# A graph network on one core: the order within a tick of the node sweeps

## The chip, the core and the metric
The kernel runs on one core of one Trainium2 chip. A core has five engines with a queue of instructions each: TensorE (matmuls; PE, and PEld for its weight loads), VectorE (DVE), ScalarE (ACT), GpSimd (POOL) and SyncE (SP, transfers only). They meet only through semaphores. The metric is the device time of one execution in microseconds; less is better. Three runs of the kernel before gave 10204.31, 10207.6 and 10220.76 us.

## The reference
Node features x [6250, 64] and 200000 edges go through four residual blocks, each `x = x + block(h)` with `h = relu(layernorm(x))`. The first block is a message-passing network of three layers:

```python
def _ffn(x, w, b):
    return jax.nn.relu(_ln(x @ w + b))
for l in range(3):
    m = concatenate([x[dst], x[src], edge_features])
    m = _ffn(m, msg_w1[l], msg_b1[l])
    m = _ffn(m, msg_w2[l], msg_b2[l])
    agg = segment_sum(m, dst)
    x = x + _ffn(concatenate([x, agg]), upd_w[l], upd_b[l])
```

The other blocks are a gated graph convolution with a batch norm, a plain sum over neighbours, and a linear message with a linear read-out. The change concerns the last line of the loop above, the update of the nodes.

## The kernel before
Nodes lie in SBUF as 49 windows of 128 nodes: H (the block's x), ACC (the aggregate) and X (the outer x), each [128, 49, 64] in float32. The kernel is a row of stages with a barrier between them. Edge work is done in spread stages and message passes; between them stand the node sweeps. node_sweep(l) is called four times: l = 0 (no update), l = 1 and 2 after the first and second message pass, and l = 3 after the third, ahead of the gate. In the texts the last three are sweeps 1, 2 and 3. The windows are cut into 7 chunks, six of 8 windows and one of a single window.

A sweep is a software pipeline whose order is written out by hand. In tick T each engine runs the pieces of its function `tick` in the order of the code, and `part(lag)` gives chunk T - lag, or nothing if there is none. The links of one chunk are:

- TensorE turns H and ACC (L1613, lag 0); ScalarE copies both out of PSUM (L1669, lag LU = 1); TensorE multiplies them with the update's weights (L1636, lag 1); VectorE adds the bias into t_pre (L1725, lag 1, two instructions, "the update's sums").
- With lag LA = 2: ScalarE squares t_pre (L1684), VectorE sums the squares of a row (L1730), ScalarE takes the root (L1686), VectorE the reciprocal (L1732) and the relu with its scale (L1735), GpSimd adds the result to H (L1797).
- In sweep 3 only, lag LN = 3: GpSimd has added H to X (L1800), and VectorE and ScalarE normalize X into H (L1742, L1744, L1746, L1693, L1749, L1695, L1751, L1753).
- TensorE turns the new H; ScalarE copies it (L1676); TensorE multiplies it with the next stage's weights (L1622, "table products"); VectorE adds the bias (L1768, "table sums"); ScalarE, GpSimd and VectorE split the result into three bf16 pieces (L1712 first, L1809 and L1699 second, L1760 third). Sweep 3 does the same for a second table (L1708, L1776, L1702, L1814).

t_pre and relu have two buffers each. The square goes into `stage`, which is one buffer for both norms, so a square waits until the earlier row sum has read it. up_ps, the update's product, has one buffer.

Of the kernel before, what the change touches and what calls it, by code (L numbers as in the profile page):

```python
# [10 lines left out]
ALU = mybir.AluOpType  # L11
ACT = mybir.ActivationFunctionType
# [5 lines left out]
D = 64  # L18
E16, E32 = 16, 32
HID = 128  # L20
LAYERS = 3
# [34 lines left out]
def build(nc, x, src, dst, ea16, ea32, w1, b1, w2, b2, wu, bu, wf, bf, ws, bs, gamma, beta, v1_in, c1, v2, c2, out):  # L56
# [23 lines left out]
    with ctx:  # L80
# [37 lines left out]
        biases = sb("biases", [P, 3 * LAYERS, D])  # L118
# [61 lines left out]
        def at_least(eng, s, value, scale=1):  # L180

            if isinstance(value, int) and value <= 0:
                return
            eng.wait_ge(s, value * scale)
# [1354 lines left out]
        def node_sweep(l, far=None, loads=None):  # L1539

            update, normed, gate = l > 0, l in (0, LAYERS), l == LAYERS
            width = 2 * D
            LU, LA, LN = 1, 2, 3 if update else 0
# [7 lines left out]
            with ExitStack() as stack:  # L1551
                def tiles(name, shape, dt=F32, slots=2):
                    return [stack.enter_context(nc.sbuf_tensor(f"{name}{h}_n{l}", shape, dt)) for h in range(slots)]

                s = {n: sem(f"node_{n}_n{l}") for n in (
                    "h_turned", "acc_turned", "h_t", "acc_t", "updated", "t", "t_square", "t_sum", "t_root", "t_rec", "relu",
                    "h_next", "x_next", "x_sum", "x_mean", "x_centre", "x_square", "x_sum2", "x_root", "x_rec", "h", "hn_turned",
                    "hn_t", "near", "near_in", "near0", "near_rest", "near1", "near2", "far", "far0", "far_in", "far1", "far2",
                    "zeroed")}
                if update:  # L1560
                    h_t, acc_t = tiles("h_t", [P, WIN // 2, P]), tiles("acc_t", [P, WIN // 2, P])
                    t_pre, relu = tiles("t_pre", [P, WIN, D]), tiles("relu", [P, WIN, D])
# [11 lines left out]
                def windows_of(i):  # L1574
                    a, b = CHUNKS[i]
                    return slice(a, b), b - a

                def sides(nw):

                    return [(e, (nw + 1 - e) // 2) for e in range(2) if nw > e]  # L1580
# [12 lines left out]
                def over_windows(v, n, f):  # L1593
                    return v.rearrange("p (a f) -> p a f", a=1).broadcast_to([P, n, f])
# [65 lines left out]
                @block.scalar  # L1660
                def _(act):
                    def tick(part):
                        if update and (i := part(LU)) is not None:
                            at, nw = windows_of(i)
                            cols, deep = (nw + 1) // 2, min(nw, 2) * D
                            for side, ps, turned, done in ((h_t, h_ps, "h_turned", "h_t"), (acc_t, acc_ps, "acc_turned", "acc_t")):
                                act.wait_ge(s[turned], i + 1)
                                at_least(act, s["updated"], i - 1)
                                act.activation(side[i % 2][0:deep, 0:cols, :].rearrange("p k n -> p (k n)"), ps[0:deep, 0:cols * P],  # L1669
                                               ACT.Copy).then_inc(s[done], 1)  # L1670
                        if (i := part(LB)) is not None:
                            at, nw = windows_of(i)
                            cols, deep = (nw + 1) // 2, min(nw, 2) * D
                            act.wait_ge(s["hn_turned"], i + 1)
                            at_least(act, s["far" if gate else "near"], i - 1)
                            act.activation(hn_t[i % 2][0:deep, 0:cols, :].rearrange("p k n -> p (k n)"), hn_ps[0:deep, 0:cols * P],  # L1676
                                           ACT.Copy).then_inc(s["hn_t"], 1)
                        if update and (i := part(LA)) is not None:
                            at, nw = windows_of(i)
                            act.wait_ge(s["t"], 2 * i + len(sides(nw)))  # L1680
                            at_least(act, s["t_sum"], i)
                            if normed:
                                at_least(act, s["x_sum2"], i - 1)
                            act.activation(square[:, 0:nw, :], t_pre[i % 2][:, 0:nw, :], ACT.Square).then_inc(s["t_square"], 1)  # L1684
                            act.wait_ge(s["t_sum"], i + 1)
                            act.activation(t_size[:, at], t_size[:, at], ACT.Sqrt, bias=eps[:], scale=1.0 / D).then_inc(s["t_root"], 1)  # L1686
                        if normed and (i := part(LN)) is not None:
                            at, nw = windows_of(i)
                            act.wait_ge(s["x_centre"], i + 1)
                            at_least(act, s["x_sum2"], i)  # L1690
                            if update:
                                act.wait_ge(s["t_sum"], min(i + 2, len(CHUNKS)))
                            act.activation(square[:, 0:nw, :], centre[:, 0:nw, :], ACT.Square).then_inc(s["x_square"], 1)  # L1693
                            act.wait_ge(s["x_sum2"], i + 1)
                            act.activation(x_size[:, at], x_size[:, at], ACT.Sqrt, bias=eps[:], scale=1.0 / D).then_inc(s["x_root"], 1)  # L1695
                        if (i := part(LB + 2)) is not None:
                            at, nw = windows_of(i)
                            act.wait_ge(s["near_rest"], i + 1)
                            act.activation(piece(at, 1), halves(near_rest[i % 2], nw), ACT.Copy).then_inc(s["near1"], 1)  # L1699
                            if gate:  # L1700
                                act.wait_ge(s["far_in"], 2 * i + len(sides(nw)))
                                act.activation(NEARB[:, at, 1, :], far_rest[i % 2][:, 0:nw, :], ACT.Copy).then_inc(s["far1"], 1)  # L1702
                        if (i := part(LB)) is not None:
                            at, nw = windows_of(i)
                            if gate:
                                act.wait_ge(s["far"], i + 1)
                                for e, n in sides(nw):
                                    act.activation(NEARB[:, at.start + e:at.stop:2, 0, :],  # L1708
                                                   far_ps[e][:, 0:n * width].rearrange("p (k f) -> p k f", f=width),
                                                   ACT.Copy).then_inc(s["far0"], 1)  # L1710
                            act.wait_ge(s["near_in"], 2 * i + len(sides(nw)))
                            act.activation(piece(at, 0), halves(near_sum[i % 2], nw), ACT.Copy).then_inc(s["near0"], 1)  # L1712

                    ticks(tick)

                @block.vector
                def _(dve):
                    def tick(part):
                        if update and (i := part(LU)) is not None:
                            at, nw = windows_of(i)  # L1720
                            dve.wait_ge(s["updated"], i + 1)
                            at_least(dve, s["relu"], i - 1)
                            at_least(dve, s["t_square"], i - 1)
                            for e, n in sides(nw):
                                dve.tensor_tensor(t_pre[i % 2][:, e:nw:2, :], up_ps[e][:, 0:n * D].rearrange("p (k f) -> p k f", f=D),  # L1725
                                                  over_windows(biases[:, 2 * LAYERS + l - 1, :], n, D), ALU.add).then_inc(s["t"], 1)
                        if update and (i := part(LA)) is not None:
                            at, nw = windows_of(i)
                            dve.wait_ge(s["t_square"], i + 1)
                            dve.tensor_reduce(t_size[:, at], square[:, 0:nw, :], AX, ALU.add).then_inc(s["t_sum"], 1)  # L1730
                            dve.wait_ge(s["t_root"], i + 1)
                            dve.reciprocal(t_size[:, at], t_size[:, at]).then_inc(s["t_rec"], 1)  # L1732
                            dve.wait_ge(s["t_rec"], i + 1)
                            at_least(dve, s["h_next"], i - 1)
                            dve.scalar_tensor_tensor(out=relu[i % 2][:, 0:nw, :], in0=t_pre[i % 2][:, 0:nw, :], scalar=0.0,  # L1735
                                                     in1=by_window(t_size[:, at], nw), op0=ALU.max,
                                                     op1=ALU.mult).then_inc(s["relu"], 1)
                        if normed and (i := part(LN)) is not None:
                            at, nw = windows_of(i)
                            if update:  # L1740
# [1042 lines left out]
```

## Time and profile before

| | us |
|---|---|
| median of three runs | 10207.6 |
| profiled execution | 10204.8 |
| its span | 10203.1 |
| TensorE busy | 7656.1 (75%) |
| GpSimd busy | 7272.0 (71%) |
| VectorE busy | 6637.9 (65%) |
| ScalarE busy | 6204.9 (61%) |

The profile is one execution. The span runs from its first to its last instruction. Busy shares are means over all stages. An engine's idle time is put down to what ended it. The mean granted clock of TensorE over the whole span is 0.809 of 2.4 GHz.

### The profile page before, as it was taken

The numbers are of one execution on the slowest core, as the hardware profiler recorded it, in microseconds if no ns is written. First come the engines' busy times: TensorE is split into PE (matmuls) and PEld (weight loads), VectorE is DVE, ScalarE is ACT, GpSimd is POOL, SyncE is SP. The second block draws the span as 40 slices with busy tenths as digits, with TensorE's granted clock in tenths as the row PEclk, the third lists the DMA queues.
The fourth block names the chain that finished last, engine by engine and source line by source line (L and its number), as shares of the span: only waits on it lengthen the run. The fifth ranks groups of instructions, "written<-read, shape, count | busy, mean of one in ns | idle before, by whom it ended". The sixth has DMA issues, their size and how long they took to land. (4 is left out here: it accounts for less than half of the span.)

```text
span 10203.1 us, 372978 instructions
## 1 busy us (share of the span) xinstructions
PE 7656.1 (75%) x123409; PEld 6557.4 (64%) x123409; DVE 6637.9 (65%) x16063; ACT 6204.9 (61%) x15877; POOL 7272.0 (71%) x10039
## 2 busy tenths in 40 slices
PE   6666666645568999978999899996888866545666
PEld 5444444434457788878888788886766656445666
DVE  7444444456645888835888358884399993664697
ACT  2555555546535999926999369983388872443343
POOL 2777777777756888846887468874589975775676
PEclk8555555556589999989999899997999989557887
DMA  5111111149998777768777687777998869667887
GB/s 229 56 56 56 59 56 55 56 131 289 284 259 299 231 237 236 231 239 290 235 230 209 248 287 235 230 204 202 385 279 270 270 184 360 209 207 241 301 255 195
DMA packets 1598119, 2189.50 MB, mean 215 GB/s; under 512 B 508971, under 2 KB 1110844, under 8 KB 1583294
## 3 DMA queue, kind: packets, MB, share of 16 engines
q1 hardware_dynamic: 1275038, 1195.71, 39.0%
q0 software_dynamic: 210528, 491.24, 17.4%
q10 hardware_dynamic: 112320, 499.48, 12.3%
q8 instruction: 141, 2.31, 0.1%
q14 instruction: 92, 0.75, 0.0%
HBM read 1245.73 MB, written 827.61 MB: 203 GB/s over the span
## 5 line engine op out<-in xcount | busy, mean ns | idle before, releaser
L636 POOL DMA_INDIRECT by_src<-sort_rec,slots x1560 | 1534.5, 984 | 650.1 <-issue 649.5
L1306 POOL DMA_INDIRECT NEAR<-spread_f,gather_ids_l x1368 | 1351.7, 988 | 252.2 <-issue 173.8
L1432 ACT ACTIVATE z_l<-z_l,sizes_l 128x64 f32<-128x64 f32 x5472 | 1375.8, 341 | 0.0
L770 PE MATMUL bank<-hots_t 104*128 104x512 bf16 (+3 forms) x1568 | 610.0, 464 | 720.1 <-ACT junk L597 719.4
L770 PEld LDWEIGHTS bank<-hots_t 104*128 104x128 bf16 x1568 | 216.5, 138 | 1017.7 <-ACT junk L597 830.8
L1516 PE MATMUL bank<-wm_diag,zr_t_l 128*128 128x128 f32 x5472 | 794.1, 288 | 0.0
L1516 PEld LDWEIGHTS bank<-wm_diag,zr_t_l 128*128 128x128 f32 x5472 | 663.6, 191 | 155.7 <-issue 155.7
L1469 PE MATMUL bank<-m_l,hot_wide_l 128*128 128x64 f32 x5472 | 744.3, 279 | 0.0
L1149 POOL COPY unit_near_a<-NEARB 128x192 bf16 x1368 | 417.4, 351 | 430.1 <-PE bank_bf L1134 221.8
L1495 PE MATMUL bank<-near_of_l,hot_t_l 128*128 128x64 bf16 x16416 | 600.8, 194 | 97.4 <-issue 54.2
L1469 PEld LDWEIGHTS bank<-m_l,hot_wide_l 128*128 128x128 f32 x5472 | 667.6, 192 | 0.0
L1495 PEld LDWEIGHTS bank<-near_of_l,hot_t_l 128*128 128x128 fp8e4 x16416 | 569.3, 99 | 143.7 <-issue 135.4
L597 ACT ACTIVATE junk<-bank,minus_one 128x512 bf16<-128x512 f32 (+2 forms) x1176 | 636.4, 541 | 26.2 <-PE bank L772 0.7
L1162 ACT ACTIVATE unit_rows_a<-bank 128x256 f32<-128x256 f32 x684 | 247.8, 384 | 618.8 <-PE bank L1134 574.1
L967 POOL DMA_INDIRECT by_dst<-move_run,target x456 | 502.6, 1102 | 143.3 <-issue 133.5
L1331 POOL TENSOR_TENSOR rest_l<-m_l 128x256 f32<-128x256 f32 x684 | 420.7, 615 | 251.0 <-DVE m_l L1400 245.3
L1182 DVE COPY unit_rows_a<-bank 128x256 f32<-128x256 f32 x513 | 205.3, 424 | 599.3 <-PE bank L1134 599.1
L619 ACT ACTIVATE sort_rec<-st 128x128 f32<-128x128 f32 x196 | 61.3, 313 | 853.6 <-DMA by_src<-sort_rec,slots 853.5
L2503 POOL DMA_INDIRECT NEAR<-spread_f,last_ids x456 | 451.0, 989 | 132.8 <-issue 111.1
L2503 POOL DMA_INDIRECT NEAR<-spread_f,sum_ids x456 | 433.2, 950 | 132.4 <-issue 119.9
L2604 PE MATMUL bank<-NEAR,sum_dst_hot 128*128 128x64 bf16 x3648 | 286.0, 234 | 320.0 <-DVE sum_last_of L2551 320.0
L2564 ACT ACTIVATE bank<-NEAR 128x512 f32<-128x512 f32 x456 | 255.1, 592 | 433.8 <-DMA NEAR<-spread_f,sum_ids 298.5
(392 smaller groups left out, 27643.5 us busy)
## 6 DMA issues: line engine op xcount, KB each, us to landing
spread_f<-unit_rows_a ACTq DMA_DIRECT2D x342, 512.0 KB, 5.9
hot_wide_l<-dst_wide SPq DMA_DIRECT2D x456, 256.0 KB
unit_hot_a<-src_hots_t SPq DMA_DIRECT2D x342, 256.0 KB, 4.1
near_of_l<-NEARB SPq DMA_DIRECT2D x1368, 48.0 KB
dst_hots<-NEAR SPq DMA_DIRECT2D x228, 256.0 KB
dst_wide<-hot_wide_l SPq DMA_DIRECT2D x228, 256.0 KB
hot_t_l<-dst_hots_t SPq DMA_DIRECT2D x456, 128.0 KB
NEAR<-dst_hots SPq DMA_DIRECT2D x456, 128.0 KB
```

Source lines behind the costliest of these rows:

```text
L597: act.activation(junk[t][:], compared(u, t), ACT.Relu, bias=minus_one[:], accum_out=rank[h][:, 4 * u + t:4 * u + t + 1]).then_inc(s["ranke ...
L636: pool.indirect_dma_start(out=by_src, out_offset=bass.IndirectOffsetOnAxis(ap=slots[h][:, j:j + 1], axis=0), in_=rec[h][:, j, :], in_offse ...
L770: pe.matmul(to, lhsT=cols[:, t * P:width], rhs=cols[:, 0:width], start=True, stop=False, skip_group_check=True)
L967: pool.indirect_dma_start(out=by_dst, out_offset=bass.IndirectOffsetOnAxis(ap=target[h][:, g:g + 1], axis=0), in_=run[h][:, g, :], in_offs ...
L1149: pool.tensor_copy(near_of[h][:, g, :, :], NEAR_FAR[:, bass.ds(w[g], 1), 1, :, :] .rearrange("p a q f -> p (a q) f")).then_inc(s["near"], 1)
L1306: pool.indirect_dma_start(out=far_in[h % WA][:, g * GT:(g + 1) * GT, :].rearrange("p j f -> p (j f)"), out_offset=None, in_=spread_f, in_o ...
L1331: pool.tensor_tensor(rest[h % 2][:], m[h % WA][:, 0:SPLIT, :], top(m[h % WA])[:, 0:SPLIT, :], ALU.subtract).then_inc(s["rest"], 1)
L1432: last = act.activation(z[h % WA][:, t, :], z[h % WA][:, t, :], ACT.Relu, scale=sizes[h % WA][:, 2, 0, t:t + 1])
L1469: last = pe.matmul(BA[h % 2][:, D:2 * D], lhsT=hot_wide[h % WA][:, j, :], rhs=m[h % WA][:, GT + j, :], start=j == 0, stop=j == GT - 1)
L1495: last = pe.matmul(BH[:, t * D:(t + 1) * D], lhsT=hot_t[h % WA][:, t, :], rhs=near_of[h % WA][:, t // GT, q * D:(q + 1) * D], start=q == 0 ...
L1516: last = pe.matmul(bank[:, q * P:(q + 1) * P], lhsT=zr_t[h % 2][:, q, :], rhs=wm2_diag[:, l, :], start=False, stop=True, skip_group_check= ...
L2503: pool.indirect_dma_start(out=rows_in[h][:, g * GT:(g + 1) * GT, :].rearrange("p j f -> p (j f)"), out_offset=None, in_=spread_f, in_offse ...
```

## The change
Two pieces of code are moved within a tick, in ScalarE's and in VectorE's function. ScalarE's square of t_pre goes from behind the copies to the head of the tick. VectorE's row sum, reciprocal and relu go ahead of the update's sums. The instructions, their operands and their waits stay.

```diff
                 @block.scalar
                 def _(act):
                     def tick(part):
+                        if update and (i := part(LA)) is not None:
+                            at, nw = windows_of(i)
+                            act.wait_ge(s["t"], 2 * i + len(sides(nw)))
+                            at_least(act, s["t_sum"], i)
+                            if normed:
+                                at_least(act, s["x_sum2"], i - 1)
+                            act.activation(square[:, 0:nw, :], t_pre[i % 2][:, 0:nw, :], ACT.Square).then_inc(s["t_square"], 1)
                         if update and (i := part(LU)) is not None:
...
                         if update and (i := part(LA)) is not None:
                             at, nw = windows_of(i)
-                            act.wait_ge(s["t"], 2 * i + len(sides(nw)))
-                            at_least(act, s["t_sum"], i)
-                            if normed:
-                                at_least(act, s["x_sum2"], i - 1)
-                            act.activation(square[:, 0:nw, :], t_pre[i % 2][:, 0:nw, :], ACT.Square).then_inc(s["t_square"], 1)
                             act.wait_ge(s["t_sum"], i + 1)
...
                 @block.vector
                 def _(dve):
                     def tick(part):
-                        if update and (i := part(LU)) is not None:
-                            at, nw = windows_of(i)
-                            dve.wait_ge(s["updated"], i + 1)
-                            at_least(dve, s["relu"], i - 1)
-                            at_least(dve, s["t_square"], i - 1)
-                            for e, n in sides(nw):
-                                dve.tensor_tensor(t_pre[i % 2][:, e:nw:2, :], up_ps[e][:, 0:n * D].rearrange("p (k f) -> p k f", f=D),
-                                                  over_windows(biases[:, 2 * LAYERS + l - 1, :], n, D), ALU.add).then_inc(s["t"], 1)
                         if update and (i := part(LA)) is not None:
...
+                        if update and (i := part(LU)) is not None:
+                            (the same eight lines)
                         if normed and (i := part(LN)) is not None:
```

VectorE's queue in sweep 3, tick 4, first as it was. t_pre0 and t_pre1 are the two buffers (chunk 3 in t_pre1, chunk 2 in t_pre0); `_n3` names the sweep.

```order
L1725 TENSOR_TENSOR t_pre1_n3<-bank2,biases 128x4x64
L1725 TENSOR_TENSOR t_pre1_n3<-bank3,biases 128x4x64
L1730 TENSOR_REDUCE small<-stage 128x8
L1732 RECIPROCAL small<-small 128x8
L1735 SCALAR_TENSOR_TENSOR relu0_n3<-t_pre0_n3,small 128x512
L1742 TENSOR_REDUCE small<-X 128x8
L1744 TENSOR_SCALAR small<-small 128x8
```

And the same place in the changed program, whose lines from there on carry other numbers:

```order
L1724 TENSOR_REDUCE small<-stage 128x8
L1726 RECIPROCAL small<-small 128x8
L1729 SCALAR_TENSOR_TENSOR relu0_n3<-t_pre0_n3,small 128x512
L1738 TENSOR_TENSOR t_pre1_n3<-bank2,biases 128x4x64
L1738 TENSOR_TENSOR t_pre1_n3<-bank3,biases 128x4x64
L1744 TENSOR_REDUCE small<-X 128x8
L1746 TENSOR_SCALAR small<-small 128x8
```

The two sums went behind the three instructions of the earlier chunk; the norm of X follows the sums directly.

ScalarE's queue in sweep 1, tick 7, before. h_t, acc_t and hn_t are the copies of turned rows, `small` the sizes, NEARB the pieces.

```order
L1669 ACTIVATE h_t0_n1<-bank0 64x128
L1669 ACTIVATE acc_t0_n1<-bank1 64x128
L1676 ACTIVATE hn_t1_n1<-bank_bf 128x512
L1684 ACTIVATE stage<-t_pre1_n1 128x512
L1686 ACTIVATE small<-small,eps 128x8
L1699 ACTIVATE NEARB<-NEAR 128x16x64
L1712 ACTIVATE NEARB<-NEAR 128x16x64
```

The same in the changed program:

```order
L1669 ACTIVATE stage<-t_pre1_n1 128x512
L1676 ACTIVATE h_t0_n1<-bank0 64x128
L1676 ACTIVATE acc_t0_n1<-bank1 64x128
L1683 ACTIVATE hn_t1_n1<-bank_bf 128x512
L1688 ACTIVATE small<-small,eps 128x8
L1701 ACTIVATE NEARB<-NEAR 128x16x64
L1714 ACTIVATE NEARB<-NEAR 128x16x64
```

The square passed three copies; the root kept its place.

## Rows read from the trace of the kernel before

**Rows 1.** Busy time by stretch, the three sweeps: stretch, length, busy time, clock, DMA.
```profile
4342.90:4419.10 76.20, 49.06 (x369) 43.78 (x369) 32.55 (x54) 27.67 (x49) 25.92 (x21) 0.57 0.00 1
5612.40:5688.80 76.40, 49.10 (x369) 43.83 (x369) 32.55 (x54) 27.78 (x49) 25.91 (x21) 0.57 0.00 1
6880.80:7005.20 124.40, 62.56 (x467) 56.06 (x467) 69.36 (x112) 46.18 (x83) 49.38 (x35) 0.58 0.48 3
```

**Rows 2.** Waits, sweep 3: who waited for whom, total us, times, longest.
```profile
DVE t_pre_n L1725 <- PE bank L1636: 32.2, 7, 7.9
...
ACT small L1686 <- DVE small L1730: 23.3, 7, 4.7
```

**Rows 3.** Timeline, sweep 1, ticks 2 and 3: start, duration, instruction, idle time ahead.
```profile
4355.66 0.76 DVE L1725 TENSOR_TENSOR t_pre_n<-bank,biases 128x256 f32<-128x256 f32 x2 [5.55 <-PE bank L1636]
...
4356.46 1.06 PE L1613 MATMUL bank<-ident,ACC 128*128 128x128 f32 x4
...
4357.25 0.58 ACT L1669 ACTIVATE h_t_n<-bank 128x512 f32<-128x512 f32 x1
...
4357.73 0.59 ACT L1669 ACTIVATE acc_t_n<-bank 128x512 f32<-128x512 f32 x1
```

**Rows 4.** Timeline, sweep 1, ticks 4 and 5.
```profile
4366.69 1.13 PE L1622 MATMUL bank<-wtab,hn_t_n 64*128 64x128 f32 x16
4366.92 0.76 DVE L1725 TENSOR_TENSOR t_pre_n<-bank,biases 128x256 f32<-128x256 f32 x2 [2.15 <-PE bank L1636]
...
4369.48 1.28 DVE L1768 TENSOR_TENSOR NEAR<-bank,table_bias 128x512 f32<-128x512 f32 x2
...
4376.37 2.05 PE L1622 MATMUL bank<-wtab,hn_t_n 64*128 64x128 f32 x16
...
4376.64 0.76 DVE L1725 TENSOR_TENSOR t_pre_n<-bank,biases 128x256 f32<-128x256 f32 x2 [5.88 <-PE bank L1636]
...
4379.20 1.28 DVE L1768 TENSOR_TENSOR NEAR<-bank,table_bias 128x512 f32<-128x512 f32 x2
```

**Rows 5.** Timeline, sweep 1, ticks 6 and 8.
```profile
4386.36 0.76 DVE L1725 TENSOR_TENSOR t_pre_n<-bank,biases 128x256 f32<-128x256 f32 x2 [5.88 <-PE bank L1636]
...
4389.02 1.23 DVE L1760 TENSOR_TENSOR NEARB<-NEAR,NEARB 128x1024 bf16<-128x1024 f32 x1
4390.17 1.28 DVE L1768 TENSOR_TENSOR NEAR<-bank,table_bias 128x512 f32<-128x512 f32 x2
...
4401.74 2.13 POOL L1809 TENSOR_TENSOR NEAR<-NEAR,NEARB 128x1024 f32<-128x1024 f32 x1
...
4401.91 3.04 DVE L1760 TENSOR_TENSOR NEARB<-NEAR,NEARB 128x1024 bf16<-128x1024 f32 x1 [0.52 <-ACT NEARB L1699]
```

**Rows 6.** Timeline, sweep 3, tick 4, and L1744 in tick 8.
```profile
6907.53 0.69 PE L1636 MATMUL bank<-wupd,h_t_n 64*128 64x64 f32 x4 [5.67 <-ACT h_t_n L1669]
...
6911.30 0.75 DVE L1725 TENSOR_TENSOR t_pre_n<-bank,biases 128x256 f32<-128x256 f32 x2 [3.88 <-PE bank L1636]
...
6913.86 0.68 DVE L1742 TENSOR_REDUCE small<-X 128x8 f32<-128x512 f32 x1
...
6914.58 0.74 DVE L1744 TENSOR_SCALAR small<-small 128x8 f32<-128x8 f32 x1
...
6967.96 0.19 DVE L1744 TENSOR_SCALAR small<-small 128x8 f32<-128x8 f32 x1
```

**Rows 7.** Timeline, turning of H; L1753's durations, ns min/median/max, starts, forms.
```profile
6932.71 1.09 PE L1613 MATMUL bank_bf<-ident,H 128*128 128x128 f32 x4 [6.13 <-DVE NEAR L1776]
...
L1753 DVE SCALAR_TENSOR_TENSOR H<-stage_t,small x14: 225/693/1764, 2861.1 to 6981.3; 128x512 f32<-128x512 f32 x12, 128x64 f32<-128x64 f32 x2
```

**Rows 8.** Busy time by stretch, sweep to sweep; timeline, sweep 1, tick 5.
```profile
4342.90:5612.40 1269.50, 1185.36 (x20661) 1062.26 (x20661) 872.11 (x1886) 956.79 (x3018) 897.53 (x1446) 0.96 0.78 242
5612.40:6880.80 1268.40, 1188.97 (x20662) 1066.12 (x20662) 872.74 (x1886) 956.99 (x3018) 897.60 (x1446) 0.95 0.77 242
...
4372.92 0.69 PE L1636 MATMUL bank<-wupd,h_t_n 64*128 64x64 f32 x4 [3.63 <-ACT h_t_n L1669]
```

More of the change, by code:

```diff
@@ L1737, in tick @@
                                                      op1=ALU.mult).then_inc(s["relu"], 1)
+                        if update and (i := part(LU)) is not None:
+                            at, nw = windows_of(i)
+                            dve.wait_ge(s["updated"], i + 1)
+                            at_least(dve, s["relu"], i - 1)
+                            at_least(dve, s["t_square"], i - 1)
+                            for e, n in sides(nw):
+                                dve.tensor_tensor(t_pre[i % 2][:, e:nw:2, :], up_ps[e][:, 0:n * D].rearrange("p (k f) -> p k f", f=D),
+                                                  over_windows(biases[:, 2 * LAYERS + l - 1, :], n, D), ALU.add).then_inc(s["t"], 1)
                         if normed and (i := part(LN)) is not None:
```

## The prediction
> **What bounds the kernel now.** I read the page first: no engine is busy for more than 75% of the span, so the kernel is a row of stages with limits of their own. The change touches node_sweep only where there is an update: the sweeps after the first and the second message pass (sweeps 1 and 2) and the one ahead of the gate (sweep 3). Second view, busy time by stretch: these three take 76.2, 76.4 and 124.4 us, together 277 us or 2.7% of the span; no engine is busy for more than 65% of any of them, and the granted clock is 0.57 to 0.58, so TensorE is mostly at 1.2 GHz [rows 1]. A barrier stands at each end of a stage, so a microsecond less in a sweep is one less in the span; outside the sweeps no instruction changes. Third view, the waits of sweep 3: VectorE waits 32.2 us for the update's products, ScalarE 23.3 us for the row sums of squares [rows 2]. That is one ring: copies (ScalarE), update matmuls (TensorE), bias sums and the rest of the tick (VectorE), and ScalarE's last instruction, which frees it for the next tick's copies. The timeline gives each link.
>
> I call T a tick's number from 0 and S the start of the update's sums (L1725) in it. The sums in tick T are those of chunk T-1; the update's norm in it is for chunk T-2.
>
> **What moves.** Nothing is added or removed. Row sum, reciprocal and relu need nothing of tick T's update, but stand behind its sums; after the change they can run while TensorE multiplies. VectorE now waits, ahead of the sums, for the square (first in ScalarE's tick) and for the root (behind ScalarE's copies). Two terms are opposed: three VectorE instructions leave the ring, the square enters it. On ScalarE a 128x512 instruction holds up the next by 0.48 us (4357.25 to 4357.73), so the square costs 0.48 [rows 3]. Is the cover long enough? The update occupies TensorE for 6911.30 - 6907.53 = 3.8 us [rows 6]; square, row sum, root behind the copies, reciprocal and relu need about 3 us from the head of the tick, and the update starts only after square and two copies, 0.48 us each. Yes, but for a last chunk of one window.
>
> **Term A, ticks 2 and 3 (no table products yet).** Before, the next tick's second copy starts 4357.73 - 4355.66 = 2.07 after S. After, sums 0.79, square 0.48 and first copy 0.48 would allow 1.75, but the turned ACC rows end at 4356.46 + 1.06 = 4357.52, so some 1.89 after S [rows 3]. Gain 0.18; two ticks each in sweeps 1 and 2, one in sweep 3: 5 x 0.18 = 0.9 us.
>
> **Term B, ticks 4 and 5 of sweeps 1 and 2.** The table sums (L1768) start 4369.48 - 4366.92 = 2.56 after S. With the three instructions gone they could start at S + 0.67, but the table products are late next: they end at 4366.69 + 1.13 = 4367.82 in tick 4, and at 4376.37 + 2.05 = 4378.42 in tick 5, where the clock is low. I take starts of 4367.9 and 4378.5 against 4369.48 and 4379.20: 1.6 and 0.7, minus the square's 0.48: 1.1 and 0.2 [rows 4]. Two sweeps: 2.6 us.
>
> **Term C, ticks 6 to 8 of sweeps 1 and 2.** In tick 6 the third pieces (L1760, 1.15 from start to start) stand between relu and table sums, which start at 4390.17 - 4386.36 = 3.81 after S. After: 0.67 + 1.15 = 1.82, and products at the low clock allow 1.85, so 1.96 less 0.48, 1.5 [rows 5]. A second effect comes in. GpSimd's H addition comes sooner, and with it the long subtraction behind it (L1809, 2.13 us), which may now run under the third pieces. With L1809 begun 0.17 us ahead, L1760 took 3.04 us instead of 1.23 [rows 5]. Bounds: 0 to 1.8 a tick; I take 0.4, nearest to an overlap at the end alone, since relu is over about 1.5 us ahead of the sums and addition and subtraction together take 3.4. So 1.1 in tick 6. Tick 7 has the same links with sums of one window and a shorter cover: I take 0.8, in tick 8 (no sums) 0.35. Together 2.25 a sweep, 4.5 us.
>
> **Term D, sweep 3.** Behind relu stands the whole norm of X, with two trips to ScalarE. Before, its first sum (L1742) starts 6913.86 - 6911.30 = 2.56 after S; after, 0.67: 1.89. Moreover L1744 took 0.74 us there, beside GpSimd's H addition, and 0.19 where it ran after that; the addition now lies under the update, so 0.55 more. Less the square: 1.96 each in ticks 3 and 4, 3.9 us [rows 6]. Tick 5: the same 2.44, but the update behind it waits for the turning of H, 6932.71 + 1.09 us, which the square only overruns by 0.3: 2.1 [rows 7]. Tick 6: the same 2.1 and 1.07 more, as L1753 took 1.76 us beside L1809 where its median is 0.69 [rows 7]; but L1809 now meets L1744 to L1746. From below that costs nothing, from above L1809's whole 2.13. I take 1.1, half: 2.1. Tick 7: one window of update covers little, so relu is late; I take 1.3 from the order and 0.6 net of contention, 1.9. Tick 8: 0.5. Together 10.5 us.
>
> Of that contention the Trainium skill (SBUF — State Buffer, Who interferes with whom) says that whichever of VectorE and GpSimd starts first keeps their shared ports for its whole instruction while the other blocks. The rows for L1760 and L1753 agree. By that rule GpSimd's earlier work moves the loss rather than ending it, and if GpSimd were always first, terms C and D would shrink as in the case "contention".
>
> **Sum.** 0.9 + 2.6 + 4.5 + 10.5 = 18.5 us: 3.9 in each of sweeps 1 and 2, 10.7 in sweep 3. The profiled execution took 10204.8 us (span 10203.1), so 10186.3. It lies 2.8 us under the median of the three runs (10207.6), which themselves span 16.5 us; for a median I add 2: 10188 us. A measurement of this kernel can tell about 0.2% (20 us) from no change; 18.5 is 0.18%.
>
> **Rivals.**
> Contention: L1809 gets in first everywhere. Then the remaining 1.2 of 1.8 is lost in ticks 6 and 7 of two sweeps (4.8), 0.8 each in ticks 6 and 7 of sweep 3 (1.6), and the 0.55 of three ticks is not won (1.7): 8 less, gain 10.5, time 10196. For it: 3.04 us [rows 5]. Against: in ticks 3 to 5 of sweep 3 there is no L1809 at all.
> Clock: shorter gaps let TensorE be granted 2.4 GHz in more ticks. Tick 4's products took 1.13 us, tick 5's 2.05, and tick 5 began with a gap of 3.63 us on TensorE [rows 4, 8]. With gaps about 1 us shorter, some ticks' update and products could run at the high clock, which would be worth half of 3.8, less what is hidden, about 1.8 a tick: five ticks, 9 us, gain 27.5, time 10179. Against: from 4372.92 to 4378.42 TensorE ran in one piece and stayed at 1.2 GHz.
> The skill (TensorE: Matmul & The Clock Gate, What's actually happening) warns that the change-over varies from run to run; no run here shows that yet.
> Nothing: something that I take for hidden ends each tick, and only the square is felt. Gain 0 to 5, time 10204.
> Slower: the high clock is lost, not won. The head square puts 0.48 us more ahead of each update's copies. Tick 4 of sweeps 1 and 2 and parts of ticks 5 and 6 in sweep 3 are above 1.2 GHz; losing all is about 9 us, not enough. The passes behind the sweeps must start lower too: they take 1269.5 and 1268.4 us with their sweeps at 0.96 and 0.95 of the clock and TensorE busy for 1185 us and more [rows 8]. A clock lower by 0.02 there is 2% of 2 x 1187, 48 us: 10204.8 - 18.5 + 9 + 48 = 10243. It decides from about 0.005 on. Against: those two stretches, alike in work, differ by 1.1 us.
>
> **Chances.** Forecast (gain 14 to 23: 10182 to 10194) 0.62, of which 0.27 lies beyond 0.2%; contention 0.15; clock 0.15; nothing 0.04; slower 0.04. So faster 0.27 + 0.15 = 0.42, same 0.35 + 0.15 + 0.04 = 0.54, slower 0.04. Range: from the clock case with a little more, 10176, to the contention case with the runs' own spread, 10203; the forecast alone 10182 to 10194.
>
> **What would show it.** Sweeps 1 and 2 at about 72.4 us each and sweep 3 at 113.7. From the start of the sums to that of L1742 in ticks 3 and 4 of sweep 3 0.7 us instead of 2.56, and L1744 at 0.19. ScalarE's wait for the row sum (23.3 us in sweep 3) nearly gone. For contention: third pieces, L1746 or L1744 at 2 us or more in ticks 6 and 7. For the clock: over 0.62 in the sweeps. I am wrong if the sweeps together shorten by less than 10 or more than 26 us, or if a pass between them changes by more than 2 us.

## The result, and the profile after

| | before | after |
|---|---|---|
| median of the runs compared, us | 10207.6 (22 runs) | 10186.5 (22 runs) |
| lowest to highest, us | 10190.9 to 10220.8 | 10157.1 to 10204.9 |
| ratio after to before, 95% interval | | 0.9978 (0.9972 to 0.9985) |
| profiled execution, span, us | 10203.1 | 10179.0 |
| sweeps 1, 2 and 3, us | 76.1, 76.3, 122.7 | 71.8, 71.8, 112.5 |
| all three, us | 275.2 | 256.2 |

The change gains 22 us, 15 to 29 by the interval: 0.22%. The 0.2% (20 us) below which I had said "no change" lies inside that interval, so the whole time alone can't say on which side of it the change falls. The forecast was 10188, inside its range. A sweep is measured here from its first turning of H to the end of its last third piece, so that the two kernels are cut at the same instructions.

Busy time by stretch, after (columns as in [rows 1]), the three sweeps:

```profile
4343.20:4415.10 71.90, 48.05 (x369) 42.81 (x369) 34.35 (x54) 27.43 (x49) 24.91 (x21) 0.57 0.00 1
...
5605.90:5677.80 71.90, 47.96 (x369) 42.72 (x369) 34.57 (x54) 27.43 (x49) 24.90 (x21) 0.57 0.00 1
...
6870.90:6983.50 112.60, 63.68 (x467) 57.06 (x467) 66.33 (x110) 45.59 (x83) 47.01 (x35) 0.56 0.53 3
```

The sweeps are shorter by 4.3, 4.5 and 10.2 us (the third stretch of [rows 1] runs 1.7 us past the last third piece), with no engine much less busy and nearly the same granted clock (0.57, 0.57, 0.56 after; 0.57, 0.57, 0.58 before). Less was waited, not less done.

The waits of sweep 3, after (us in total, times, longest):

```profile
ACT stage L1695 <- DVE stage_t L1748: 31.0, 6, 7.0
...
DVE t_pre_n L1738 <- PE bank L1636: 19.9, 6, 7.9
...
DVE small L1726 <- ACT small L1688: 5.7, 7, 1.8
...
ACT small L1688 <- DVE small L1724: 0.2, 1, 0.2
```

ScalarE's wait for the row sum (23.3 us in [rows 2]) is down to 0.2. VectorE's wait for the update fell from 32.2 to 19.9: it fills that time with row sum, reciprocal and relu, at the price of a wait of 5.7 us for the root, which lies under the update. ScalarE is not busier for it: its idle time now stands at the square of X's norm (31.0 us, 19.4 before).

The timeline of sweep 3, tick 4, after (start, duration, instruction, idle time ahead):

```profile
6893.88 0.61 ACT L1669 ACTIVATE stage<-t_pre_n 128x512 f32<-128x512 f32 x1
6894.40 0.57 ACT L1676 ACTIVATE h_t_n<-bank 128x512 f32<-128x512 f32 x1
...
6895.56 0.69 PE L1636 MATMUL bank<-wupd,h_t_n 64*128 64x64 f32 x4 [3.73 <-ACT h_t_n L1676]
...
6896.26 0.69 DVE L1729 SCALAR_TENSOR_TENSOR relu_n<-t_pre_n,small 128x512 f32<-128x512 f32 x1
...
6897.03 1.27 POOL L1799 TENSOR_TENSOR H<-H,relu_n 128x512 f32<-128x512 f32 x1 [6.57 <-DVE relu_n L1729]
...
6899.28 0.76 DVE L1738 TENSOR_TENSOR t_pre_n<-bank,biases 128x256 f32<-128x256 f32 x2 [2.32 <-PE bank L1636]
6899.95 0.68 DVE L1744 TENSOR_REDUCE small<-X 128x8 f32<-128x512 f32 x1
6900.66 0.17 DVE L1746 TENSOR_SCALAR small<-small 128x8 f32<-128x8 f32 x1
```

The square starts, and 0.52 us later the first copy; relu is over 2.3 us before the sums; the norm's first sum (now L1744) starts 0.67 us after the update's sums instead of 2.56, and L1746 (L1744 before) takes 0.17 instead of 0.74, since GpSimd's H addition is over by then [rows 6] (6897.03 + 1.27 against 6900.66).

The same kernel, sweep 3, ticks 6 and 7: GpSimd's long subtraction and what VectorE ran beside it.

```profile
6921.69 2.13 POOL L1811 TENSOR_TENSOR NEAR<-NEAR,GATEB 128x1024 f32<-128x1024 f32 x1
...
6922.61 1.70 DVE L1746 TENSOR_SCALAR small<-small 128x8 f32<-128x8 f32 x1
...
6936.44 2.13 POOL L1811 TENSOR_TENSOR NEAR<-NEAR,GATEB 128x1024 f32<-128x1024 f32 x1
...
6937.34 1.77 DVE L1755 SCALAR_TENSOR_TENSOR H<-stage_t,small 128x512 f32<-128x512 f32 x1
```

A [128, 8] operation of 0.17 us took 1.70 in tick 6, and in tick 7 the product that writes H took 1.77 (its median was 0.69 [rows 7]). Each ends 0.5 us behind the subtraction (6924.31 against 6923.82, 6939.11 against 6938.57): the loss moved, it did not go. So the engines of this kernel meet in more than their semaphores: no semaphore stands between these pairs, and the later one is held up.

### The profile page after: what moved, and what is told of

Read it like the earlier page. It is cut to its first block and busy times, and to the rows that moved or that the text cites. A ratio compares the mean times of both kernels' runs of the same rounds, so it can differ in the third digit from the quotient of the medians.

```text
span 10179.0 us, 372978 instructions
## 1 busy us (share of the span) xinstructions
PE 7649.8 (75%) x123409; PEld 6551.4 (64%) x123409; DVE 6643.5 (65%) x16063; ACT 6203.9 (61%) x15877; POOL 7270.8 (71%) x10039
## 3 DMA queue, kind: packets, MB, share of 16 engines
q8 instruction: 141, 2.31, 0.1%
## 5 line engine op out<-in xcount | busy, mean ns | idle before, releaser
L1495 PEld LDWEIGHTS bank<-near_of_l,hot_t_l 128*128 128x128 fp8e4 x16416 | 569.9, 99 | 135.2 <-issue 126.4
L1162 ACT ACTIVATE unit_rows_a<-bank 128x256 f32<-128x256 f32 x684 | 247.8, 384 | 620.2 <-PE bank L1134 585.3
```

The lines of the kernel that those rows point to most:

```text
L1495: last = pe.matmul(BH[:, t * D:(t + 1) * D], lhsT=hot_t[h % WA][:, t, :], rhs=near_of[h % WA][:, t // GT, q * D:(q + 1) * D], start=q == 0 ...
```

## The experiments

Each line of "sweeps" is 1, 2, 3 and their sum, in us, from one profile. Of one and the same kernel two profiles differed by 0.5 us (the change) and by 3.4 us (e3) in this sum. The before of a ratio ran on the same chip. e4b, e5, e6 and e6b were run once each, so only their sweeps are read.

**The two halves.** Theory: neither half brings the whole, as row sum and relu ahead of the sums need the square early.

e1_square_only. VectorE keeps the old order, ScalarE's square goes to the head:

```
 vector tick:  update's sums   <- back ahead of row sum, reciprocal, relu
 scalar tick:  square, h_t/acc_t copies, hn_t copy, root   (as after)
```

> Only ScalarE's half of the change: the square of t_pre heads the tick, VectorE keeps its old order. The three sweeps, from the first turning of H to the last third piece, take 275.2 us before (76.1, 76.3, 122.7) and 256.2 us after (71.8, 71.8, 112.5). Ring theory (the square stands ahead of the copies that release the update, and nothing leaves VectorE's part of the ring): 0.3 to 0.5 us more in each tick that has copies, the three sweeps together 277 to 281 us, whole time slower by 2 to 6 us, too little to be told in the time of the whole kernel. Rival (an earlier square lets the row sum go earlier, and this is where the gain of the change comes from): sweeps at 265 us or less.

Sweeps 77.0, 76.6, 124.2, together 277.8: 2.6 more than before. Ratio 1.0008 (0.9999 to 1.0018). Waits of its sweep 3:

```profile
DVE t_pre_n L1727 <- PE bank L1636: 34.1, 7, 7.9
ACT small L1688 <- DVE small L1732: 26.4, 6, 5.3
```

ScalarE waits for the row sum even longer (26.4 against 23.3), VectorE for the update too: nothing is won, and the square is felt. In sweep 3 the copies of ticks 4, 5 and 6 lie 1.0, 1.5 and 2.1 us later than before, 0.5 a tick. The sum is smaller than that, as the updates of tick 6 in sweeps 1 and 2 took 2.4 and 2.5 us instead of 3.7: TensorE was granted 2.4 GHz in more of them (0.59 and 0.61 over these sweeps).

e2_vector_only. The other half:

```
 vector tick:  row sum, reciprocal, relu, update's sums   (as after)
 scalar tick:  h_t/acc_t copies, hn_t copy, square, root  <- as before
```

> Only VectorE's half: row sum, reciprocal and relu ahead of the update's sums, the square stays behind ScalarE's copies. Theory that the halves need each other: the row sum at the head of VectorE's tick now waits for a square behind two or three copies, so relu is done 1.5 us later than in the changed kernel and holds up the sums in ticks with a short or fast update and in sweep 3; sweeps 258 to 264 us, a gain of 11 to 17 instead of 19. Rival (the update covers this too, and the square's 0.48 us a tick is saved): sweeps at 252 us or less, better than both kernels by 4 us or more.

Sweeps 73.6, 71.8, 115.3, together 260.6: 14.6 less than before. Ratio 0.9986 (0.9976 to 0.9996). So the halves are not additive: +2.6 and -14.6 make -12.0, both together -19.0; some 7 us come only from the pair, about twice what two profiles of one kernel differed by. In sweep 3 e2 is 0.3 us ahead of the full change at the copies of tick 5 (no square in the ring); at tick 6 it is 0.2 behind, at tick 8 2.3, at the end 2.8. Its sweep 3, tick 6:

```profile
6918.65 0.62 ACT L1684 ACTIVATE stage<-t_pre_n 128x512 f32<-128x512 f32 x1
...
6919.30 0.69 DVE L1722 TENSOR_REDUCE small<-stage 128x8 f32<-128x512 f32 x1 [1.98 <-ACT stage L1684]
...
6923.94 2.12 POOL L1809 TENSOR_TENSOR NEAR<-NEAR,GATEB 128x1024 f32<-128x1024 f32 x1
...
6924.05 2.57 DVE L1746 TENSOR_TENSOR stage_t<-X,small 128x512 f32<-128x512 f32 x1
```

VectorE stands at its head 1.98 us for a square that is behind the copies; relu comes late, with it GpSimd's addition and subtraction, and the subtraction meets the norm's 128x512 product (2.57 us) where in the full change it met a smaller loss.

**Is the price of the square 0.48, and is the cover real?** A first form of the next run, e4_square_twice, with both squares into one buffer, gave no time. e4b_square_doubled adds a second square, into a buffer that nobody reads; e6_rowsum_doubled a second row sum, likewise, where it should be hidden; e6b_rowsum_doubled_before the same on the kernel before, where it should be felt.

```
+ act.activation(spare[:, 0:nw, :], t_pre[i % 2][:, 0:nw, :], ACT.Square)          # e4b, ahead of the square
+ dve.tensor_reduce(spare[:, 0:nw], square[:, 0:nw, :], AX, ALU.add)               # e6, e6b, ahead of the row sum
```

> The changed kernel with a second square of t_pre at the head of ScalarE's tick, into a tile that nobody reads: the one cost that the change puts into the ring, doubled. Ring theory: 0.5 us more in each of the 15 ticks with a 512-wide square and copies behind it, less where the update waits for the turning of H: three sweeps 256.2 plus 5 to 8, 261 to 264 us. Rival (ScalarE has slack at the head of the tick): under 258.5.

Sweeps 74.5, 72.5, 114.7, together 261.8, 5.6 more than after. In sweep 3 the copies of ticks 2, 3 and 4 lie 0.4, 0.8 and 1.4 us later than after's. The timeline of sweep 1 shows its price, start to start:

```profile
4366.62 0.63 ACT L1670 ACTIVATE spare_n<-t_pre_n 128x512 f32<-128x512 f32 x1 [4.42 <-DVE t_pre_n L1740]
4367.15 0.61 ACT L1671 ACTIVATE stage<-t_pre_n 128x512 f32<-128x512 f32 x1
4367.67 0.58 ACT L1678 ACTIVATE h_t_n<-bank 128x512 f32<-128x512 f32 x1
```

A square holds the next instruction up by 0.52 us (a copy by 0.48), and 0.4 to 0.5 of it reaches the end of each tick. The price was right to 0.05. The sum is held down by sweep 2 (+0.7 only), whose update of tick 5 took 2.0 us instead of 3.5.

> The changed kernel with a second row sum of the square (0.68 us, into a tile that nobody reads) ahead of the first. Cover theory (the three instructions lie under the update's matmuls): nothing in most ticks, only tick 7 of each sweep, whose update has one window, and the fast ticks 4 feel it: three sweeps 256.2 plus 1 to 4. Rival (they are still in the ring, and the gain came from somewhere else): plus 0.7 in each of 18 ticks, 268 us.

Sweeps 72.3, 70.2, 111.9, together 254.4: 1.8 less than after, and 2.8 below the least that I had expected. Its timeline in sweep 1:

```profile
4360.40 0.69 DVE L1725 TENSOR_REDUCE spare_n<-stage 128x8 f32<-128x512 f32 x1 [0.70 <-ACT stage L1670]
4361.00 0.68 DVE L1726 TENSOR_REDUCE small<-stage 128x8 f32<-128x512 f32 x1
...
4365.26 0.75 DVE L1740 TENSOR_TENSOR t_pre_n<-bank,biases 128x256 f32<-128x256 f32 x2 [2.28 <-PE bank L1637]
```

The extra 0.6 us comes out of VectorE's idle time: out of the wait ahead of the sums (2.67 us in after, 2.28 left here) and out of the wait for the root. Up to the copies of tick 5 each copy starts within 0.3 us of after's. The sum is lower mainly by sweep 2, where the updates of ticks 6 and 7 took 0.5 us less each than in after.

> The kernel before with the same second row sum, where it stands behind the update's sums, in the ring. Cover theory: 0.7 us in each of 18 ticks with a full chunk, at least wherever the root or the table sums follow: three sweeps 275.2 plus 9 to 13, 284 to 288. If it cost as little here as in the changed kernel, the place of the row sum would not be what the change is about.

Sweeps 78.0, 77.6, 125.2, together 280.8, 5.6 more than before but below what I had expected. Until tick 5 the addition shows in full: the copies of ticks 3, 4 and 5 of sweep 1 lie 0.6, 1.2 and 1.8 us later. Then they catch up (1.7 at tick 6, 1.2 at tick 7), and the granted clock of these sweeps is 0.61 instead of 0.57: TensorE was at 2.4 GHz in more of the late ticks. The updates of ticks 5 and 6 of sweeps 1 and 2 together took 4.2 us less than before's; with that added the sum would be 9.8 more, inside the 9 to 13 that I had expected, but this is an estimate and no run. So the cover and the price of 0.6 are seen in the ticks without that disturbance; neither sum is by itself a measure of the row sum's price.

**Is contention a cost of its own?** e5_subtract_on_before and e3_subtract_first move GpSimd's subtraction to the head of its tick, on the kernel before and on the one after:

```
 pool tick:
+   wait near0; near_rest = near_sum - piece 0      (L1809/L1811, moved here)
    clear ACC; H += relu; X += H
-   wait near0; near_rest = near_sum - piece 0
```

> The kernel before with GpSimd's long subtraction ahead of its additions, nothing else moved. If contention with that subtraction is a cost of its own, independent of the order on VectorE and ScalarE: three sweeps 265 to 270 us instead of 275.2, mostly in ticks 6 and 7 of sweep 3 (L1753 at 0.69 instead of 1.76) and tick 8 of the others. If it bites only in the changed order, since there the subtraction comes under the norm of X: over 273.

Sweeps 73.7, 73.3, 117.9, together 264.9: 10.3 less than before, without any of the change. It is 0.1 under the lowest sum that I had expected. Of it 0.8 is the clock's: the first turning of its sweep 1 still ran at a granted clock of 0.99 instead of 0.50, and the copies of tick 1 came 1.2 us after its start instead of 2.0. The product that took 1.76 us in tick 6 of sweep 3 [rows 7] is back at its median:

```profile
6934.16 0.69 DVE L1753 SCALAR_TENSOR_TENSOR H<-stage_t,small 128x512 f32<-128x512 f32 x1
```

> The changed kernel, and in GpSimd's tick the long subtraction for the second pieces goes ahead of the H (and X) additions, so that it runs under the update and is over before VectorE's sums end. Contention theory: L1746's 1.70 us in tick 6 of sweep 3, the third pieces' 2.5 us in tick 6 of sweeps 1 and 2 and their 2.97 in tick 8 shrink to their undisturbed 0.2 and 1.23; sweeps 69.5 to 70.5 us each for 1 and 2 and 107 to 110 for 3, together 246 to 251, a further gain of 5 to 10 us over the changed kernel. Rival (GpSimd's additions, now later, are late for X's norm or block VectorE instead): together 254 us or more.

Sweeps 68.8, 69.1, 106.6, together 244.5: 11.6 less than after, 30.7 less than before, and 1.5 under the lowest that I had expected; ratio 0.9977 (0.9967 to 0.9987). Its sweep 3:

```profile
6915.65 2.13 POOL L1798 TENSOR_TENSOR NEAR<-NEAR,GATEB 128x1024 f32<-128x1024 f32 x1 [6.94 <-ACT GATEB L1714]
...
6922.78 0.69 DVE L1755 SCALAR_TENSOR_TENSOR H<-stage_t,small 128x512 f32<-128x512 f32 x1
...
6931.55 0.69 DVE L1748 TENSOR_TENSOR stage_t<-X,small 128x512 f32<-128x512 f32 x1
```

The subtraction starts as soon as its operand is there, while VectorE waits for ScalarE or TensorE, and the products of X's norm are back at 0.69 us in each tick with a full chunk. The move also lets ScalarE's second pieces start earlier, so the gain need not all be contention. VectorE's busy time tells how much is: with the same instructions it falls from 132.8 to 124.5 us in the three sweeps on the kernel before, and from 135.2 to 124.7 on the one after, 8.3 and 10.5 us of the gains of 10.3 and 11.6. The contention is thus nearly as dear in either order. The change brought 2 us of it and left the rest in place.

**Once more, for what the sweeps' gain is worth in the whole.** e3b_subtract_first_again and after_again are e3 and after, unedited, on another chip together with e7.

> The changed kernel with the subtraction first, once more, with more rounds on the same chip as its rival: its ratio to before was 0.9977 (0.9967 to 0.9987) although its sweeps are 30.6 us shorter, which is 0.9970. If the sweeps are all that counts, the ratio comes out at 0.9970 give or take 0.0005; if the shorter sweeps cost something in the stages behind them, nearer to 0.9978.

> The changed kernel itself in the same rounds. Sweeps 256.2 us again within 0.5; ratio to before 0.9978 to 0.9985 (19 us of sweeps are 0.9981); the stages between the sweeps, whose code is the same, within 3 us of the other profiles each, either way.

after_again: sweeps 71.8, 71.4, 112.5, together 255.7; ratio 0.9990 (0.9981 to 0.9999). e3b: 72.2, 69.4, 106.2, together 247.8; ratio 0.9975 (0.9965 to 0.9986). The sweeps of the changed kernel repeat within 0.5 us, those of e3 within 3.4. The whole repeats less well: 0.9990 here against 0.9978 with 22 runs, two intervals that overlap from 0.9981 to 0.9985. Pass 2 took 1195.9 us in after_again and 1190.9 in after, the same code, so my 3 us for it was too narrow, and the ratio of 0.9990 is outside the 0.9978 to 0.9985 that I had expected. Whether all of the sweeps' gain arrives in the whole (0.9970 by e3's sweeps, 0.9973 by e3b's own) or a little less (0.9975 measured) stays open; the interval holds all three.

e3 and e3b also show the clock's part. The same code, the same stretch of sweep 1 (30.7 to 38.3 us from its start, tick 5), in e3 and then in e3b:

```profile
4369.80:4377.40 7.60, 6.02 (x60) 5.57 (x60) 3.80 (x8) 3.40 (x7) 4.04 (x4) 0.78 0.00 0
```

```profile
4373.26:4380.86 7.60, 7.05 (x59) 6.86 (x60) 3.13 (x7) 1.32 (x4) 2.89 (x3) 0.54 0.00 0
```

The update of one tick in either, e3 first:

```profile
4370.34 0.44 PE L1636 MATMUL bank<-wupd,h_t_n 64*128 64x64 f32 x4 [1.26 <-ACT h_t_n L1676]
```

```profile
4373.81 0.69 PE L1636 MATMUL bank<-wupd,h_t_n 64*128 64x64 f32 x4 [1.27 <-ACT h_t_n L1676]
```

The gap ahead of it is the same (1.26 and 1.27 us), the products take 0.44 us in the one and 0.69 in the other (granted clock over the update 1.00 and 0.50, that is 2.4 and 1.2 GHz), and sweep 1 is 68.8 against 72.2 us. Over the whole of sweep 1 both stand at 0.57, so the mean clock of a sweep does not show it. A variation of this kind, up to 3 us a sweep, is what blurred e1, e4b, e6 and e6b. The Trainium skill (TensorE: Matmul & The Clock Gate, What's actually happening) says that the moment of the change-over varies from run to run; these two profiles agree, which the traces ahead of the prediction could not show.

**A better version?** e7_root_too is e3 with ScalarE's root moved ahead of the hn copy:

```
 scalar tick:  square, h_t/acc_t copies, root, hn_t copy
```

> The changed kernel with the subtraction first (which measured 244.5 us for the three sweeps and 10180.5 us) and the root of the update's norm ahead of ScalarE's copy of the turned new H, so that it no longer waits for that turning (in tick 7 of sweep 3 the root stood behind a copy that waited 0.53 us, in tick 8 behind one that waited 1.23). Theory: relu comes 0.4 to 0.9 us sooner in ticks 4 to 8, which counts only where the update is short or fast: sweeps 241 to 244 us, whole time 10176 to 10186, not to be told from the former, but clearly under before. Rival (the root, waiting for the row sum, holds up the copy and with it the table products): 246 us or more.

Sweeps 69.9, 70.6, 105.5, together 245.9 (0.7 less in sweep 1 by a first turning at the high clock, as in e5): between the two theories, which had stood at 244 or less and 246 or more. Ratio 0.9966 (0.9955 to 0.9977). Its sweep 1, tick 7:

```profile
4398.56 0.30 ACT L1681 ACTIVATE small<-small,eps 128x8 f32<-128x8 f32 x1 [0.43 <-DVE small L1724]
4398.77 0.58 ACT L1687 ACTIVATE hn_t_n<-bank_bf 128x512 f32<-128x512 f32 x1
```

Sweep 3 gains 1.2 over e3 and 0.8 over e3b, but sweep 2 loses 1.1 to 1.5: in tick 7 the root waits 0.43 for the row sum and holds up the copy that the table products need; the copy of tick 8 is 1.6 to 2.0 us later than in e3 and e3b. About half of that is contention again: ScalarE's second pieces stand behind that copy, so VectorE's third pieces start late (5663.16), behind GpSimd's H addition (5662.95), and take 2.15 us instead of e3's 1.21. e7 and e3 both beat before and after in the sweeps; between the two no run decides, as their ratios overlap.

## Why the prediction was right

The copies at a tick's head date the ring. What had been gained by then, forecast against measured, in us (start of the copy of turned ACC rows; from tick 8 on of turned new H):

| gained by | tick 3 | 4 | 5 | 6 | 7 | 8 | end |
|---|---|---|---|---|---|---|---|
| sweep 1, forecast | 0.2 | 0.4 | 1.5 | 1.7 | 2.8 | 3.6 | 3.9 |
| measured | 0.2 | 0.3 | 1.1 | 1.4 | 2.5 | 3.8 | 4.3 |
| sweep 3, forecast | 0.2 | 2.1 | 4.1 | 6.2 | 8.3 | 10.2 | 10.7 |
| measured | 0.2 | 2.1 | 4.1 | 6.2 | 7.8 | 9.8 | 10.2 |

**Term A**: 1.0 us over the five ticks instead of 0.9.

**Term B**: 1.1 instead of 1.3 a sweep. **Term C**: 2.9 instead of 2.25, and one size in it right by two errors. Sweep 1, after, ticks 4 to 6:

```profile
4366.98 1.11 PE L1622 MATMUL bank<-wtab,hn_t_n 64*128 64x128 f32 x16
4367.19 0.76 DVE L1738 TENSOR_TENSOR t_pre_n<-bank,biases 128x256 f32<-128x256 f32 x2 [0.43 <-PE bank L1636]
...
4368.14 1.29 DVE L1770 TENSOR_TENSOR NEAR<-bank,table_bias 128x512 f32<-128x512 f32 x2 [0.19 <-PE bank L1622]
...
4375.41 2.08 PE L1622 MATMUL bank<-wtab,hn_t_n 64*128 64x128 f32 x16
...
4377.53 1.29 DVE L1770 TENSOR_TENSOR NEAR<-bank,table_bias 128x512 f32<-128x512 f32 x2 [1.06 <-PE bank L1622]
...
4381.50 0.44 PE L1636 MATMUL bank<-wupd,h_t_n 64*128 64x64 f32 x4 [1.76 <-ACT h_t_n L1676]
...
4384.34 2.13 POOL L1811 TENSOR_TENSOR NEAR<-NEAR,NEARB 128x1024 f32<-128x1024 f32 x1
4384.35 0.76 DVE L1738 TENSOR_TENSOR t_pre_n<-bank,biases 128x256 f32<-128x256 f32 x2 [1.31 <-PE bank L1636]
4385.02 2.53 DVE L1762 TENSOR_TENSOR NEARB<-NEAR,NEARB 128x1024 bf16<-128x1024 f32 x1
4387.48 1.27 DVE L1770 TENSOR_TENSOR NEAR<-bank,table_bias 128x512 f32<-128x512 f32 x2
```

Ticks 4 and 5: the table products are late next, as said: L1770 waits 0.19 and 1.06 us for them and starts 0.95 and 1.8 after the sums (L1738), against 2.56 in both before [rows 4]. What B lacks is of the size of what the clock took: in tick 4 the update began at 1.2 GHz, and from its start to the sums it was 2.29 us (4364.90 to 4367.19) instead of 2.04 (4364.88 to 4366.92). Tick 6: the subtraction (L1811) began 0.68 ahead of the third pieces (L1762), which took 2.53 instead of 1.23: 1.3 lost where I had put 0.4. But the first half of that tick's update ran at 2.4 GHz (0.44 instead of 0.69 for four products), so that from its start to the sums 2.85 us went instead of 3.7 in tick 5 of before (4372.92 [rows 8] to 4376.64 [rows 4]; tick 6 of before was the same): 0.9 given back. Net 1.0, against a forecast of 1.1: here luck. Tick 7 gave 1.3 where I had 0.8; there the third pieces (L1762) kept their 1.21 us, and it was GpSimd's H addition, begun 0.02 us after them, that took 2.31 instead of 1.27.

**Term D**: ticks 3 to 5 are right to 0.1, with the two sizes that they rest on, 0.67 and 0.17, seen above. Tick 6 gained 1.7 instead of 2.1: the subtraction took 1.5 from L1746 where I had put 1.1. Tick 7 brought the sum to 9.8 of 10.2; counted from the copies of ACC that is 1.9, from those of the new H 1.4, against my 1.9. The 0.6 of it that I had put as won from contention was not won (L1755 took 1.77, L1753 before 1.76).

So 19.0 us came where I had 18.5: over all sweeps A gave 0.1 more, B 0.3 less, C 1.2 more and D 0.5 less. Part of C is not the order's: the updates of sweeps 1 and 2 took 0.7 and 1.0 us less in all than before's, by the clock that tick 6 was granted. By that estimate the order itself is worth 17.3, still within 10% of the forecast.

**The whole.** The profiled span fell by 24.1, of which 19.0 in the sweeps. The other 5.1 lie in stages whose instructions are the same: ahead of the sweeps +0.3, pass 2 -2.5, pass 3 +1.2, behind sweep 3 -4.1. Over all the profiles of this study pass 2, pass 3 and the stretch behind sweep 3 took 1189.7 to 1195.9, 1188.4 to 1198.9 and 3195.5 to 3202.1 us, whatever stood in the sweeps, so 5.1 lies within their spread, and nothing shows it to be an effect of the change. My bound that a pass should not change by more than 2 us was too narrow: pass 2 changed by 2.5, and by that sign I would have called a right prediction wrong. That the whole came within 1.5 us of 10188 is in part luck, as single runs of the changed kernel range over 48 us; the sweeps are the test.

**The rivals.** Contention: part right. Third pieces at 2.53, L1746 at 1.70 and L1755 at 1.77 are its signs, but in ticks 3 to 5 of sweep 3 there was nothing to meet, and in tick 6 it took 0.9 (sweeps 1 and 2) and 0.4 (sweep 3) more than I had put, not 8 us in all. The Trainium skill (SBUF — State Buffer, Who interferes with whom), by which the engine that starts first keeps the ports, agrees with these rows: the subtraction kept its 2.13 us each time, and the loser, begun 0.1 to 0.9 us behind it, ended only after it. What I had not seen is how cheaply the loss could be won back: e5 gives about 10 us on the kernel before. Clock: not in the means (0.57, 0.57, 0.56), but in one half of an update in tick 6 of sweeps 1 and 2, worth the 1.7 us above and not 9. after_again stood at 0.62, 0.60, 0.56 with the same lengths within 0.4 us, so the mean clock says little there. Nothing: refuted by the sweeps. Slower: the passes did not change beyond their spread; their granted clock is 0.99 and 0.98, against 0.98 in both before.

The one weak spot is the chances. The sum stood at 0.18%, at the edge of 0.2%, and the whole's spread of some us decides on which side a result falls: 0.9978 (0.9972 to 0.9985) in one comparison, 0.9990 (0.9981 to 0.9999) in the other. The chances of 0.42 and 0.54 said as much.

## What to carry to other kernels

Follow the ring through its queues, and date each tick by one instruction of it: an operation that stands behind a wait it does not need is moved ahead, and its whole duration comes back while the next late operand allows it (here 1.9 us a tick where nothing was next, and 0.7 to 1.6 us less the square's 0.5 where the table products were). A shortened ring shifts when GpSimd and VectorE meet; look at each long elementwise operation of GpSimd and start it where VectorE waits, which here was worth 11.6 us beside the change's 19.0, for one moved block. Judge such a change by ticks ahead of any change of clock, and not by one sum.

## What the runs showed of the hardware

The mean granted clock of the page (0.81 after, 0.91 in e3) says nothing of the time here. In the first 2000 us TensorE was granted 0.55 before and 1.00 in e3, in code that is the same:

```profile
0.00:2000.00 2000.00, 1277.16 (x10260) 879.03 (x10260) 1028.60 (x3704) 959.58 (x2867) 1395.12 (x1437) 0.55 0.24 78
```

```profile
0.00:2000.00 2000.00, 1287.00 (x10260) 886.61 (x10260) 1032.68 (x3704) 959.58 (x2867) 1394.73 (x1437) 1.00 0.24 78
```

TensorE's busy time is 1277.2 and 1287.0 us, the commonest matmul there (L760, 2888 of them) has a median of 0.28 us in both, so the operations did not get shorter by the clock that the profile states, and sweep 1 began at 4342.9 and 4339.1 us. Why, the traces do not tell.

A tiny operation can pay the full price of contention: 1.70 us for a [128, 8] tensor_scalar of 0.17. Operations that stood beside GpSimd's subtraction and kept their time were the sums out of PSUM (L1738 at 4384.35, 0.76 us) and the reduction (L1744 at 6921.90, 0.68).
